# Group norms of both images in one sequence, and the second norm from sums of x y

## The reference

```
x = x + L0(gn(x), W_cat, W_scale, gamma, beta)
x = x + L1(gn(x), codebook)
x = x + L2(gn(x), Wk, bk)
x = x + L3(gn(x), ...)

L0: guidance = conv3x3(x, W_cat)              # 45 channels
    for d in (1, 6, 12, 24, 36):
        w = softmax(guidance[9 of 45]); outs += sum of 9 shifted x * w, dilation d
    y = conv1x1(concat([x] + outs), W_scale)
    L0 = (y - mean(y)) * rsqrt(var(y) + eps) * gamma + beta    # per channel, over both images
L1: for each pixel the nearest of 8192 codes
L2: depthwise 3x3 with kernels made from the image's mean
L3: two deformable 3x3 convolutions, each with group norm and relu
```

## Time and profile before

| | us |
|---|---|
| median of 3 runs | 1700.38 |
| lowest and highest | 1697.67, 1702.74 |
| the profiled execution | 1702.24 |
| its span, first to last instruction | 1700.4 |
| TensorE busy | 1312.0 |
| VectorE busy | 1156.8 |
| GpSimd busy | 999.7 |
| ScalarE busy | 416.2 |

### The profile page before, as it was taken

One profiled execution on the slowest core, in us unless ns is written; L12 is line 12 of the kernel. 1 busy time (PEld: TensorE's weight loads), 2 busy tenths in 40 slices (PEclk: granted clock), 3 DMA queues, 4 the chain that ended last, 5 costly groups with the idle time before them and its releaser, 6 DMA issues.

```text
span 1700.4 us, 22882 instructions
## 1 busy us (share of the span) xinstructions
PE 1312.0 (77%) x7855; PEld 913.7 (54%) x7898; DVE 1156.8 (68%) x1477; ACT 416.2 (24%) x1287; POOL 999.7 (59%) x979
## 2 busy tenths in 40 slices
PE   5888999488998888679855599687667867676675
PEld 2345555244444444334435578666567666666675
DVE  4667678679999999998966947544455444554444
ACT  2241000213343432333431132222112212121111
POOL 4256568222344442325776877777777777777772
PEclk9889999789999999889976799799898989877877
DMA  4041000011111111133474597787777878776773
GB/s 151 25 161 39 2 0 0 0 45 38 45 32 57 57 52 30 32 104 113 133 232 131 163 291 240 212 247 246 232 226 210 266 229 248 209 233 211 210 210 115
DMA packets 111112, 232.84 MB, mean 137 GB/s; under 512 B 14676, under 2 KB 60500, under 8 KB 110748
## 3 DMA queue, kind: packets, MB, share of 16 engines
q0 software_dynamic: 58176, 191.30, 37.4%
q1 hardware_dynamic: 52828, 40.17, 7.5%
HBM read 205.15 MB, written 26.26 MB: 136 GB/s over the span
## 4 chain that ended last, share of the span: by engine, by line
POOL 29%; PE 23%; issue 16%; DVE 11%; ACT 1%; DMA 0%; another core or an unknown queue 0%; POOLq 0%; DVEq 0%; ACTq 0%
POOL code_region L1843 11%; POOL max_region L1843 6%; POOL early_region L1843 5%; POOL late_region L1843 5%; PE score L1249 5%; PE score L1250 5%; PE score L1248 5%; DVE max_region L1650 3%; PE score L1271 3%; DVE x L267 2%; PE turn_ps L1152 1%; PE turn_ps L1280 1%; DVE code_region L1686 1%; PE score L1182 1%; DVE n_stats L152 1%
## 5 line engine op out<-in xcount | busy, mean ns | idle before, releaser
L1650 DVE SCALAR_TENSOR_TENSOR max_region<-score,nc,max_region 128x512 f32<-128x512 f32 x504 | 347.6, 740 | 37.5 <-PE score L1250 35.2
L1843 POOL DMA_INDIRECT code_region<-corners,lead_region x252 | 251.9, 999 | 76.6 <-issue 75.4
L1686 DVE TENSOR_TENSOR code_region<-score,code_region 128x4608 f32<-128x4608 f32 x28 | 138.8, 4957 | 125.2 <-DMA code_region<-corners,lead_region 124.9
L675 POOL TENSOR_TENSOR prod_acc<-prod_acc,prod_pool 128x752 f32<-128x752 f32 (+8 forms) x112 | 149.0, 1330 | 107.0 <-DVE prod_pool L648 99.6
L1271 PE MATMUL score<-ident,code_region 128*128 128x128 f32 x1008 | 146.0, 316 | 56.5 <-DVE code_region L1686 56.5
L1271 PEld LDWEIGHTS score<-ident,code_region 128*128 128x128 f32 x1008 | 140.3, 167 | 61.1 <-DVE code_region L1686 59.8
L1843 POOL DMA_INDIRECT early_region<-corners,lead_region x136 | 133.1, 979 | 41.3 <-issue 40.8
L1443 ACT COPY code_region<-score 128x384 f32<-128x384 f32 x144 | 68.8, 479 | 361.6 <-PE score L1271 361.5
L1843 POOL DMA_INDIRECT max_region<-corners,lead_region x130 | 123.4, 949 | 39.6 <-issue 39.3
L1843 POOL DMA_INDIRECT late_region<-corners,lead_region x126 | 119.4, 948 | 43.7 <-issue 37.8
L1761 POOL DMA_INDIRECT late_region<-code_rows,block_id x35 | 37.8, 1081 | 157.6 <-DVE block_id L1497 99.0
(11 more groups left out here) (210 smaller groups left out, 2561.8 us busy)
## 6 DMA issues: line engine op xcount, KB each, us to landing
corners<-lead_region SPq DMA_DIRECT2D x72, 192.0 KB, 4.4
corners<-lead_region SPq DMA_DIRECT2D x8, 576.0 KB, 7.1
code_rows<-codes_n SPq DMA_DIRECT2D x8, 516.0 KB, 4.2
codes_t<-in_codes_t SPq DMA_DIRECT2D x8, 512.0 KB, 3.6
codes_n<-in_codes SPq DMA_DIRECT2D x8, 512.0 KB, 4.5
code_region<-corners,lead_region POOLq DMA_INDIRECT x252, 3.7
x<-in_x SPq DMA_DIRECT2D x2, 1152.0 KB, 6.6
out<-x SPq DMA_DIRECT2D x4, 576.0 KB, 3.2
```

What stands on the lines that cost most here:

```text
L675: pool.tensor_tensor(to, to, v, ALU.add).then_inc(pooled, 1)
L1650: dve.scalar_tensor_tensor(r, score[SLOT[k]][:], nc2[:, m:m + 1], r, ALU.add, ALU.max).then_inc(dve_took, 1)
L1686: dve.tensor_tensor(q4, bc(wps[:, u * n:(u + 1) * n], P), q4, ALU.mult).then_inc(weighted, 1)
L1843: pool.indirect_dma_start(quad(T, k), None, table[j].rearrange("n s c -> n (s c)"), bass.IndirectOffsetOnAxis(index[j % B][:, at:at + 1], 0))\
```

## The change

- `begin` and `inv_sqrt` are gone. `Opening` runs in the block of `guidance`: the moments of image 0 and of image 1, one matmul on [128, 4], one chain of small operations with two columns, one root. ScalarE writes the two halves of image 0, VectorE those of image 1. The first convolution waits for the first halves, the third for the second. The loads come in another order, the codebook's transfers stand right behind them on SP's queue, and GpSimd waits with `CodeSplit` for both images.
- In `branches` VectorE takes, behind the statistics of a chunk, the sum over its columns of x y (`scalar_tensor_tensor` with an accumulated output). The statistics and the sum of image 0's last chunk stand behind the loop (`last_moments`).
- `norm_between` is gone. `Between` runs at the start of `finale`'s block: the mean and variance of the new x follow from those of x (kept by `Opening`), those of y, and the sums of x y. VectorE and ScalarE then make z, zh and zl of the first 512 columns alone, and TensorE starts the search. GpSimd does the rest: it scales y, adds it to x, and writes z, zh and zl of the other 4096 columns, in three cuts.
- SP's loads of the later layers come behind `zeroed`, since they go where y lies.

```diff
-def begin(nc, tools, x, xpad, gm32, loads):
...
+class Opening:
...
+    def sp(self, sp):
+        x, loads = self.x, self.loads
+        sp.dma_start(x[:, 0, :], loads[0][1][:, 0, :]).then_inc(self.x_in[0], 16)
+        sp.dma_start(self.gm32, loads[1][1]).then_inc(self.gm_in, 16)
+        sp.dma_start(x[:, 1, :], loads[0][1][:, 1, :]).then_inc(self.x_in[1], 16)
+        for to, array in loads[2:]:
+            sp.dma_start(to, array).then_inc(self.loaded, 16)
...
+    def pool(self, pool):
+        pool.memset(self.xpad[:], 0.0).then_inc(self.zeroed, 1)
+        for applied in self.applied:
+            pool.wait_ge(applied, 2)
...
+    def dve(self, dve, ps):
+        chain = Chain(dve, self.step)
+        var, tmp, scale = self.var[:], self.tmp[:], self.scale[:]
+        for b in range(B):
+            dve.wait_ge(self.x_in[b], 16)
+            for q in range(NCH):
+                last = dve.bn_stats(self.stats[:, b, q, :], self.x[:, b, q * CH:(q + 1) * CH])
+            chain(last)
+            chain(dve.bn_aggr(self.moments[:, b, :], self.stats[:, b].rearrange("p q s -> p (q s)")))
+        mean, square = self.moments[:, :, 0], self.moments[:, :, 1]
+        chain(dve.tensor_tensor(tmp, mean, mean, ALU.mult))
+        chain(dve.tensor_tensor(square, square, tmp, ALU.add))
+        dve.sem_inc(self.moments_ready, 1)
...
+        dve.sem_inc(self.affine, 1)
+        dve.wait_ge(self.zeroed, 1)
+        for h in range(2):
+            to, v = self.half(1, h)
+            dve.tensor_scalar(to, v, self.scale[:, 1:2], self.shift[:, 1:2], ALU.mult, ALU.add)\
+                .then_inc(self.applied[1], 1)
...
+    def pe_half(self, pe, h):
+        for applied in self.applied:
+            pe.wait_ge(applied, h + 1)
...
+        for h in range(2):
+            to, v = self.half(0, h)
+            act.activation(to, v, ACT.Identity, bias=self.shift[:, 0:1], scale=self.scale[:, 0:1])\
+                .then_inc(self.applied[0], 1)
...
+                if r in (0, H // 2 // ROWS - 1):
+                    opening.pe_half(pe, r // (H // 2 // ROWS - 1))
...
+            opening.pe(pe, gtp[0][:, 0:2 * B])
+            opening.wait_loaded(pe)
...
+                        at = b * HW + 2 * (o["q"] - 1) * CH
+                        dve.scalar_tensor_tensor(xy_each[:], y[:, bass.ds(at, 2 * CH)], 1.0,
+                                                 x_flat[:, bass.ds(at, 2 * CH)], ALU.mult, ALU.mult,
+                                                 accum_out=xy[:, bass.ds(b * CHUNKS + o["q"] - 1, 1)])
+            dve.wait_ge(y_free, 1 + CHUNKS)
+            last_moments(dve, x_flat, y, stats, xy, xy_each[:], 0)
...
+def last_moments(dve, x_flat, y, stats, xy, each, b):
+    for q in range(NCH - 2, NCH):
+        dve.bn_stats(stats[:, b * NCH + q, :], y[:, b * HW + q * CH:b * HW + (q + 1) * CH])
+    v = slice(b * HW + (NCH - 2) * CH, (b + 1) * HW)
+    at = b * (NCH // 2) + NCH // 2 - 1
+    return dve.scalar_tensor_tensor(each, y[:, v], 1.0, x_flat[:, v], ALU.mult, ALU.mult, accum_out=xy[:, at:at + 1])
...
+class Between:
...
+        chain(last_moments(dve, self.x, self.y, self.stats, self.xy, each, 1))
+        chain(dve.bn_aggr(mv, self.stats.rearrange("p q s -> p (q s)")))
+        chain(dve.tensor_scalar(mv[:, 1:2], mv[:, 1:2], EPS, None, ALU.add))
+        dve.sem_inc(self.var_ready, 1)
...
+        chain(dve.tensor_scalar(mean, mx, t, None, ALU.add))
+        chain(dve.scalar_tensor_tensor(mean, my, s, mean, ALU.mult, ALU.add))
+        chain(dve.scalar_tensor_tensor(var, vy, s, cov, ALU.mult, ALU.add))
+        chain(dve.scalar_tensor_tensor(var, var, s, prod, ALU.mult, ALU.add))
+        chain(dve.tensor_tensor(square, mean, mean, ALU.mult))
+        chain(dve.tensor_tensor(square, var, square, ALU.add))
+        dve.sem_inc(self.moments_ready, 1)
+        first = self.x[:, 0:self.FIRST]
+        chain(dve.scalar_tensor_tensor(first, self.y[:, 0:self.FIRST], s, first, ALU.mult, ALU.add))
+        gmean, gsquare = self.gg[:, :, 0], self.gg[:, :, 1]
+        dve.wait_ge(self.group_ready, 1)
...
+        dve.sem_inc(self.affine, 1)
+        chain(dve.tensor_scalar(z, first, scale[:, 0:1], self.first_shift[:, 0:1], ALU.mult, ALU.add))
+        dve.wait_ge(self.high, 1)
+        dve.tensor_tensor(zl, z, zh, ALU.subtract).then_inc(self.low, 1)
+        chain(dve.scalar_tensor_tensor(self.shift[:], gmean, -1.0, scale, ALU.mult, ALU.mult))
+        dve.sem_inc(self.shifts, 1)
...
+        pe.wait_ge(self.high, 1)
+        pe.wait_ge(self.low, 1)
...
+        act.wait_ge(self.affine, 1)
+        act.activation(zh, self.x[:, 0:self.FIRST], ACT.Identity, bias=self.first_shift[:, 0:1],
+                       scale=self.scale[:, 0:1]).then_inc(self.high, 1)
...
+        rest, x, y = self.rest, self.x, self.y
+        cuts = [(self.FIRST, HW, 0), (HW, early, 1), (early, N, 1)]
+        pool.wait_ge(self.shifts, 1)
+        pool.wait_ge(self.high, 1)
+        pool.tensor_scalar(x[:, 0:self.FIRST], x[:, 0:self.FIRST], self.t[:], None, ALU.add).then_inc(rest, 1)
+        v = slice(self.FIRST, N)
+        pool.tensor_scalar(y[:, v], y[:, v], self.s[:], self.t[:], ALU.mult, ALU.add).then_inc(rest, 1)
+        pool.wait_ge(rest, 2)
+        pool.tensor_tensor(x[:, v], x[:, v], y[:, v], ALU.add).then_inc(rest, 1)
+        pool.wait_ge(rest, 3)
+        for a, c, b in cuts:
+            z, zh, zl = places(a, c)
+            pool.tensor_scalar(z, x[:, a:c], self.scale[:, b:b + 1], self.shift[:, b:b + 1], ALU.mult, ALU.add)\
+                .then_inc(rest, 1)
+        pool.wait_ge(rest, 6)
+        for a, c, b in cuts:
+            z, zh, zl = places(a, c)
+            pool.tensor_copy(zh, z).then_inc(rest, 1)
+        pool.wait_ge(rest, 9)
+        for a, c, b in cuts:
+            z, zh, zl = places(a, c)
+            pool.tensor_tensor(zl, z, zh, ALU.subtract).then_inc(rest, 1)
+    DONE = 12
...
-                    pe.wait_ge(z1_ready, 6)
+                    pe.wait_ge(between.rest, between.DONE)
...
+            between.pool(pool, EARLY * PX, z_places)
             pool.memset(zeros, 0.0).then_inc(zeroed, 1)
...
             depthwise.sp(sp)
+            sp.wait_ge(zeroed, 1)
             for to, array in loads:
                 sp.dma_start(to, array).then_inc(loaded, 16)
-            sp.wait_ge(zeroed, 1)
...
```

280 lines of the change are left out of this document (143 added, 137 removed).

## The result

| | before | after |
|---|---|---|
| median, us | 1700.38 | 1689.33 |
| lowest and highest | 1697.67, 1702.74 | 1686.41, 1692.72 |
| profiled execution | 1702.24 | 1686.41 |
| its span | 1700.4 | 1684.6 |

The ratio is 0.9936, 95% interval 0.9920 to 0.9952: faster, by 11.05 us (8.2 to 13.6 by the interval). The forecast was 1683.2, its range 1678 to 1689; the measured median lies 0.3 above the range and 6.1 above the forecast. The two profiled executions differ by 15.8, since the one of before lies 1.9 over its median and the one of after is the shortest of its five.

The account below looks back on a forecast made before the run. No one engine was taken to bound the kernel; each stage has its own bound, with serial chains in the opening and before the search. 4.1 + 16.6 − 3.5 = 17.2 us less gave 1685.0, or 1683.2 against the median; range 1678 to 1689.

Parts of the forecast that it names:

- Opening, 4.1 forecast: Opening norms of both images: first guidance matmul at 17.5 instead of 21.60 us, 4.1 us less.
- The guidance takes nothing back: Guidance after the opening: shifted phase against GpSimd's codebook split priced at nothing, 1 us either way.
- Price of the sums: Branches' loop: each new 768-column VectorE sum 0.96 us, plus 0.62 waiting for GpSimd at the first place; 5.1 in all.
- Half rate: Rival on the sums of products: 768 columns take 1.76 us, 3.0 us more in all, 1686.2; chance 0.12 for 1685 to 1688.
- How much reaches TensorE: Branches' loop: 70 per cent of the sums' 5.1 us of VectorE delays TensorE, 3.5 us more.
- The clock at the search's start: Search's start: TensorE's clock stays at a mean of 0.53 after idling; if it did not fall, 1.6 us less.
- Between, 16.6 forecast: Between branches and search: first score matmul at 329.8 instead of 346.42 us, 16.6 us less.
- GpSimd's 32.5 us with 12 to spare: Search's start: GpSimd's remaining columns take 32.5 us, to 362.5, 12 us before the second chunk needs them; no cost.
- "The gain should reach the end.": Search and later stages: they are relative to the earlier ones, so the whole 17.2 us should arrive.
- guidance: Rival in the guidance: GpSimd's split or image 1's later landing takes back part of the opening's gain; 1685 to 1689, chance 0.12.
- Longer stalls in the loop, up to 1693: Rival in the branches' loop: longer stalls there, total up to 1693 us; chance 0.06.
- made up: Rival in the branches' loop: TensorE's 21 us of gaps absorb the inserted sums, 1679.7; chance 0.18 for 1678 to 1681.

Follow-up runs that it names:

- run 5: Changed kernel with each of the four loop sums followed by the same product without accumulation: 1930.88 us beside the changed kernel's 1925.97.
- run 1: Changed kernel without the four sums of x y in the branches' loop: 1685.02 us, ratio to before 0.9906.
- run 2: Changed kernel with the four loop sums replaced by second statistics of the same columns, one SBUF input: 1689.45 us, ratio to before 0.9935.
- run 6: Changed kernel unaltered, run again as partner: 1916.2 us (ratio to before 0.9971) and 1925.97 us (0.9948) in sets with slow gathers.
- run 7: Changed kernel with GpSimd's last step between branches and search done four times instead of once: 1928.18 us, beside 1916.2 in the same set.
- run 10: Kernel before profiled a second time, and the changed kernel, unaltered, once more beside it: 1689.72 against 1702.05 us, ratio 0.9935.
- run 8: Changed kernel with ScalarE's first copy of y ahead of the codebook's last squares: 1684.08 us, ratio to before 0.9903, beside the changed kernel's 1689.72.
- run 9: Kernel of run 8 with the statistics of y moved from VectorE to ScalarE: 1675.52 us, ratio to before 0.9844.
- run 4: Changed kernel with statistics and sums of chunks 0 and 1 taken later in the loop: 1687.0 us, ratio to before 0.992.

## Why the forecast was off, step by step

- **Opening, 4.1 forecast, 3.9 measured.** Right, term by term: root trip 0.33, matmul trip 0.80. Each half took 1.3 on ScalarE as priced; VectorE's, for which I took 1.2, took 0.84, which is off the critical path.
- **The guidance takes nothing back.** Right: 67.8 and 68.6 us from its first matmul to the first spread matmul before, 67.3 to 69.0 after.
- **Price of the sums.** Right to 0.1 us: 0.94 and 1.52 for 0.96 and 1.58. Half rate, the rival that the Trainium skill's page on VectorE suggested (Vector Engine (DVE) Microarchitecture Reference, section Points that are easy to get wrong), is refuted: by the prediction's estimate it needs 1.76 for 768 columns of float32 with an accumulated output, the row has 0.94, and the same operation without the accumulated output has 0.95 (run 5).
- **How much reaches TensorE, the step that failed.** I took 70 per cent, 3.5 us, because TensorE has 21 us of gaps in the loop and VectorE 65. The loop became 6.1 us longer, 5.7 if all four loops without sums are taken. TensorE's gaps were no slack: by the waits in the trace of before 11.4 of the 21 us end with a product of VectorE and 4.4 with ScalarE's first copy. TensorE, VectorE and GpSimd hand products round, and what delays VectorE delays the next product. Runs 1, 2 and 5 show 0.86 to 0.9 us for each 0.94, 1.35 for 1.52: 4.5 us, nine tenths of the sums' 4.92, which is 1.0 of the 2.6 us. The other 1.2 to 1.6 is for the most part TensorE's clock, a term the sum did not have at all: TensorE's busy time is 209.9 us on average with the sums, 208.9 in the two executions of before and 209.1 in all four without, and two of the five last intervals have the 1.7 us of run 6. What remains lies within the spread of the first interval. I had kept the clock as a question of the stretch between the stages only. The bounds (0 to 10.6) held; my range did not use them.
- **The clock at the search's start.** Right: 0.53 in the first 4 us, as before, and 0.57 in another execution.
- **Between, 16.6 forecast, 15.8 measured.** The block's end with its hand-over costs 0.60 from copy to statistics where it was 0.3, operations that read a scalar per partition take 0.22 for 0.16, and ScalarE's 512 columns 0.81 for the 0.69 of a row that read PSUM and wrote float32; this pass reads SBUF and writes bfloat16, and which of the two costs the 0.12 was not tested.
- **GpSimd's 32.5 us with 12 to spare.** Right: 31.1 and 14 (run 7).
- **"The gain should reach the end."** Open. I put the loss behind the search's start at nothing. 13.8 us are there on average at the first eviction, 11.05 and 12.3 in the medians, whose intervals reach 13.6 and 14.3. Whether something is lost is not shown, and no cause was found (run 10).
- **The frame.** I set the sum against the profiled execution and took off 1.9 for the median. With the stages as measured, 1700.38 less 13.8 is 1686.6; the 2.7 us from there to 1689.33 are the open point above.

Of the rivals with a mechanism of their own none was the case; the time of "guidance" (1685 to 1689) is near by accident, since the guidance took nothing. "Longer stalls in the loop, up to 1693", with a chance of 0.06 and no working, is what happened in kind, and deserved more than "made up" at 0.18.

## What to carry to other kernels

Where three engines pass work round in a loop, price every operation that is put between two of the loop's own at its full length (here nine tenths of it arrived), whatever the busy shares say, and look for an engine outside the ring: here ScalarE, 25 of 228 us busy, took 4 us of statistics for nothing. Then ask for TensorE's clock: here a stall of 1.8 us was followed by 3.0 us of slower work, one of 4.7 by 2.4. And before estimating from one pair of profiles, ask how much one stage varies between executions of one kernel; 2.8 us in this loop was half of what was being measured.

## What the runs showed of the hardware

- TensorE's granted clock falls in some intervals of the loop and not in others, in the same program and behind the same work: 0.95 against 1.00 costs 1.7 us in 35.9 (34.67 busy against 32.98). These values are means of stretches at 1.00 and at 0.50. Idle times of 3.4 to 4.7 us at the first chunk's end were followed by an interval at 0.91 to 0.93 in seven executions, and without the idle time that interval was at 1.00 in six (runs 8 and 9). One of 1.83 us was followed by one at 0.91 (run 4).
- A VectorE operation with two SBUF inputs waits for GpSimd's current accumulation (1.52 and 2.25 for 0.94). Operations with one do not: statistics at the same place take their 1.01, a product of 768 columns 0.95.
- A scalar_tensor_tensor with two float32 SBUF inputs of 768 columns takes 0.94 us with an accumulated output and 0.95 without, and the read of the accumulator 0.08 behind it.
- ScalarE adds up its output for 0.19 us more (an accumulator read behind an ACTIVATE of 0.81 for 768 columns, where the plain copy is 0.80).
- GpSimd took 1.59 us for 512 columns in place with one scalar, and 3.75 for 4096 with two: the short pass was far off the 0.9 to 1.0 ns a column that the long ones have. What held it was not looked into.
